# Attention scores in fp16 halves with a row of maxima: fp32 strips of 16 or 17 rows replaced by stacked 32-row strips

## The reference

```
x = x + tanh(g_xattn) * attention(layernorm(x), ctx, ctx)
    scores  = einsum('bkgsd,bktd->bkgst', qh, kh) / sqrt(16)
    weights = softmax(scores, axis=-1)
    out     = einsum('bkgst,bktd->bkgsd', weights, vh)
x = x + tanh(g_ffn) * moe(layernorm(x))
```

## Time and profile before

| | us |
|---|---|
| median of 3 runs | 1436.35 |
| lowest and highest | 1429.1, 1441.07 |
| the profiled execution | 1441.87 |
| its span | 1440.1 |

### The profile page before, as it was taken

The page is one execution under the profiler, slowest core; times in us unless marked ns, Lnnn a source line. Parts: engine busy times, 40 slices in busy tenths (PEclk is TensorE's granted clock), DMA queues, the critical chain, the costliest instruction groups (busy, mean ns, idle before and its releaser), DMA issues.

```text
span 1440.1 us, 33203 instructions
## 1 busy us (share of the span) xinstructions
PE 1353.0 (94%) x11762; PEld 989.7 (69%) x11762; DVE 878.3 (61%) x1737; ACT 519.9 (36%) x949; POOL 465.0 (32%) x373
## 2 busy tenths in 40 slices
PE   4789999999996889989999999999999999999996
PEld 3456666666652767777777777777777777777773
DVE  3767767777755886854545555544444444446887
ACT  2256656676653522222222222222222222222220
POOL 2147777777773700011111111111111111004454
PEclk9979989999985579999999999999999999999998
DMA  7224434444342741136255363546163631167666
GB/s 244 94 90 139 144 116 140 141 158 135 132 144 78 260 164 60 59 134 204 81 181 183 131 204 102 198 145 219 58 211 124 200 106 58 44 211 235 212 206 189
DMA packets 98782, 213.59 MB, mean 148 GB/s; under 512 B 10800, under 2 KB 12336, under 8 KB 98736
## 3 DMA queue, kind: packets, MB, share of 16 engines
q1 hardware_dynamic: 87536, 176.28, 36.0%
q0 software_dynamic: 11200, 36.71, 8.2%
HBM read 228.26 MB, written 66.06 MB: 204 GB/s over the span
## 4 chain that ended last, share of the span: by engine, by line
PE 89%; DVE 5%; issue 2%; DMA 2%; ACT 1%; POOL 1%; SPq 0%; DVEq 0%; ACTq 0%; POOLq 0%
PE PS L1351 38%; PE PS L1370 19%; PE PS L1193 8%; PE PS L1205 8%; PE PS L1215 5%; PE PS L1339 3%; PE PS L1226 3%; PE PS L1175 2%; DVE st L752 1%; DMA xnd<-xhl 1%; PE PS L1236 1%; PE PS L1296 1%; DVE negm L807 1%; POOL xhl L545 1%; PE PS L1164 1%
## 5 line engine op out<-in xcount | busy, mean ns | idle before, releaser
L1370 PE MATMUL PS<-wb,ghl 128*128 128x512 f16 x1296 | 293.1, 383 | 7.5 <-DVE ghl L1055 4.3
L1351 PE MATMUL PS<-xT,wb 128*128 128x256 f16 x2592 | 293.8, 274 | 1.1 <-DVE xT L1033 1.1
L1351 PE MATMUL PS<-uhl,wb 128*128 128x256 f16 x2592 | 291.8, 273 | 1.0 <-DVE uhl L1043 1.0
L1351 PEld LDWEIGHTS PS<-xT,wb 128*128 128x128 f16 x2592 | 254.5, 98 | 31.8 <-issue 1.3
L1351 PEld LDWEIGHTS PS<-uhl,wb 128*128 128x128 f16 x2592 | 251.4, 98 | 29.6 <-DVE uhl L1043 1.3
L807 DVE TENSOR_REDUCE negm<-PS 128x4 f32<-128x512 f32 x256 | 164.9, 686 | 117.5 <-PE PS L1193 114.9
L1370 PEld LDWEIGHTS PS<-wb,ghl 128*128 128x128 f16 x1296 | 127.8, 99 | 152.8 <-issue 14.1
L560 POOL COPY ixr<-idx 128x2 int32 x38 | 7.0, 184 | 606.9 <-PE PS L1339 478.2
L1205 PE MATMUL PS<-qT,kT 17*128 17x512 f32 x512 | 182.7, 690 | 16.5 <-ACT Pt L625 13.5
L625 ACT ACTIVATE Pt<-PS 128x512 f32<-128x512 f32 x256 | 140.1, 607 | 156.7 <-PE PS L1205 156.2
L1193 PE MATMUL PS<-kT,qT 16*128 16x128 f32 x2048 | 162.8, 300 | 8.0 <-DVE negm L807 8.0
(11 more groups left out here) (142 smaller groups left out, 1397.2 us busy)
## 6 DMA issues: line engine op xcount, KB each, us to landing
wb<-wsc SPq DMA_DIRECT2D x126, 1024.0 KB
wst<-in_wall SPq DMA_DIRECT2D x32, 768.0 KB, 5.6
wsc<-whl SPq DMA_DIRECT2D x32, 768.0 KB, 4.2
ysl<-yb SPq DMA_DIRECT2D x46, 512.0 KB
bd<-in_bdown SPq DMA_DIRECT2D x42, 256.0 KB
X<-in_x SPq DMA_DIRECT2D x8, 1024.0 KB, 8.8
xnd<-xhl SPq DMA_DIRECT2D x32, 256.0 KB, 2.9
xs<-xnd SPq DMA_DIRECT2D x32, 256.0 KB
```

The lines of the kernel that those rows point to most:

```text
L1351: ins = pe.matmul(bank[:, hf, (m % 2) * TT:(m % 2 + 1) * TT], wb[:, par, l, k, w, m * P:(m + 1) * P], rhs(x, k), start=(n == 0), stop=(n = ...
L1370: ins = pe.matmul(PS[2][:, t, :], ghl[:, x, k, t * P:(t + 1) * P], wb[:, par, 2, k, w, :], start=(n == 0), stop=(n == len(TERMS) - 1))
```

## The change

Queries and keys are split into fp16 halves. In a strip of 32 rows the queries now stand as 16 rows of the high half and 16 rows of the low half. The keys get two such strips: `w` = 0 has the high half twice, `w` = 1 has the low half in its first 16 rows. Two accumulating matmuls, over 32 rows and over 16, give the score. The maxima are a third pass over one row, a row of `negR` times a row of ones. They no longer go into `qT`.

The parts, by engine:

- PE: `tr_k` makes 4 fp16 transposes and `tr_q` 8 in one piece, where there were 2 and 4 + 4 in fp32. `scores_max` has 16 fp16 matmuls, and `scores_T` has 6 of 512 columns (3 passes for each of two strips). `m_done`, `t_done` and `exp_done` count whole units.
- DVE: `maxes` is one instruction of 1024. `evac_q1` is gone, `evac_k` copies 512 fp16 elements, and `norm1` (the normalised x in fp32) and `weights64` are new on it.
- ACT: `exps` is one instruction of 1024. `queries` becomes `high`, which writes `kx` and then the high half of `qx`, and it moves behind the first `exps`. `evac_q` copies all 1024 elements of `qT`.
- POOL: `weights64` leaves, and `split_kq` comes, which subtracts the high halves to get the low ones of keys and queries.
- Order: `evac_neg(nx, 0)` and its transpose move behind the third maximum, `outputs(pv, 1)` behind the second, `outputs(b, 0)` and `stats2` to the end of the body.

```
             def neg_rows(half, par, pair):
                 sp.wait_ge(S["negT_ready"], 2 * number(half, par) + pair + 1)
-                sp.dma_start(qT[D::STRIP, quad, pair, :, :], negT[:, pair, :]).then_inc(neg_in[pair], 16)
+                sp.dma_start(negR[0::STRIP, par, pair, :, :], negT[:, pair, :]).then_inc(neg_in[pair], 16)
...
+            def split_kq(half, par):
+                b = 2 * half + par
+                cv = C[:, bass.ds(b, 1), :].rearrange("p o (h d) -> p (o h) d", d=D)
+                need(g, S["tk_done"], b - 1)
+                g.wait_ge(S["kh_ready"], b + 1)
...
+                g.tensor_tensor(kx[:, par, 1, :, 0, :], cv, kx[:, par, 0, :, 0, :], ALU.subtract).then_inc(S["k_split"], 1)
+                g.wait_ge(S["qh_ready"], b + 1)
+                g.wait_ge(S["xn_ready"], b + 1)
+                xv = xn32[:, par, :].rearrange("p (k m d) -> p k m d", m=HPG, d=D)
+                g.tensor_tensor(qx[:, par, :, :, 1, :].rearrange("p m k d -> p k m d"), xv,
+                                qx[:, par, :, :, 0, :].rearrange("p m k d -> p k m d"), ALU.subtract).then_inc(S["q_split"], 1)
...
+            def high(half, par):
+                b = 2 * half + par
+                need(act, S["tk_done"], b - 1)
+                cv = C[:, bass.ds(b, 1), :].rearrange("p o (h d) -> p (o h) d", d=D)
+                act.activation(kx[:, par, 0, :, :, :], cv.unsqueeze(2).to_broadcast([P, NKV, 2, D]), ACT.Copy).then_inc(S["kh_ready"], 1)
+                need(act, S["tq_done"], b - 1)
+                act.activation(qx[:, par, :, :, 0, :].rearrange("p m k d -> p k m d"),
                                X[:, bass.ds(b, 1), :].rearrange("p o (k m d) -> p (o k) m d", m=HPG, d=D),
+                               ACT.Identity, bias=ln[:, 1, bass.ds(b, 1)], scale=ln[:, 0, bass.ds(b, 1)]).then_inc(S["qh_ready"], 1)
...
             def exps(half, par, u):
-                for odd in range(2):
-                    act.wait_ge(S["t_done"], 2 * n + odd + 1)
...
+                act.wait_ge(S["t_done"], n + 1)
+                act.activation(Pt[:, u, :, :].rearrange("p h s -> p (h s)"), Tb[:, :, :].rearrange("p o c -> p (o c)"), ACT.Exp,
+                               scale=float(D) ** -0.5).then_inc(S["exp_done"], 1)
...
             def body(half, par, quad):
...
+                exps(half, par, 0)
                 if after is not None:
-                    queries(*after[:2])
-                exps(half, par, 0)
+                    high(*after[:2])
...
+            def norm1(half, par):
+                b = 2 * half + par
+                need(v, S["q_split"], b - 1)
+                v.tensor_scalar(xn32[:, par, :], X[:, bass.ds(b, 1), :].rearrange("p o c -> p (o c)"), ln[:, 0, bass.ds(b, 1)],
+                                ln[:, 1, bass.ds(b, 1)], ALU.mult, ALU.add).then_inc(S["xn_ready"], 1)
...
+                v.wait_ge(S["m_done"], UNITS * b + u + 1)
+                v.tensor_reduce(negm[:, u // 2, u % 2 * 8:u % 2 * 8 + 8], Mb[:, :, :].rearrange("p o (m t) -> p (o m) t", t=CTX),
+                                AX.X, ALU.max, negate=True).then_inc(S["max_done"], 1)
...
             def scores_max(half, par, quad, u):
...
                 for m in range(HPG):
+                    for w, rows in ((0, STRIP), (1, D)):
+                        for odd in range(2):
+                            part = strip(u, odd, rows)
+                            ins = pe.matmul(Mb[:, odd, m * P:(m + 1) * P], qT[part, quad, u // 2, m, :], kT[part, quad, w, u // 2, :],
+                                            start=w == 0, stop=w == 1)
+                ins.then_inc(S["m_done"], 1)
...
             def scores_T(half, par, quad, u):
...
                 pe.wait_ge(neg_in[u // 2], 16 * (b + 1))
+                need(pe, S["exp_done"], UNITS * b + u)
+                for w, rows in ((0, STRIP), (1, D)):
+                    for odd in range(2):
+                        part = strip(u, odd, rows)
+                        pe.matmul(Tb[:, odd, :], kT[part, quad, w, u // 2, :], qT[part, quad, u // 2, :, :].rearrange("p m c -> p (m c)"),
+                                  start=w == 0, stop=False)
                 for odd in range(2):
+                    part = strip(u, odd, 1)
+                    ins = pe.matmul(Tb[:, odd, :], one16[part, :], negR[part, par, u // 2, :, :].rearrange("p m c -> p (m c)"),
+                                    start=False, stop=True)
+                ins.then_inc(S["t_done"], 1)
```

More of the change, by code:

```diff
@@ L661, in body @@
                 if after is not None:
[L662 removed]
+                    evac_q(*after)
                 exps(half, par, 2)
@@ L1262, in body @@
                 if after is not None:
-                    tr_k(*after)
-                if not start:
-                    outputs(*pv, 1)
+                    tr_k(*after[:2])
                 scores_T(half, par, quad, 1)
@@ L1282, in body @@
                     tr_neg(*nx[:2], 1)
-                if after is not None:
-                    tr_q(*after[:2], 1)
+                outputs(half, par, quad, 0)
             over_batches(pe, body)
```

189 lines of the change are left out of this document (83 added, 106 removed).

## The result

The changed kernel takes 1449.45 us (median of 14 runs, 1443.51 to 1462.95), the kernel before 1436.24 in the same session (14 runs, 1426.73 to 1441.29). The ratio is 1.0103, with a 95% interval of 1.0072 to 1.0135. So it is slower, as forecast, but by 13 us instead of 37, and the interval leaves open whether it is more than the 1% that the prediction calls tellable. The time lies inside the whole range of 1405 to 1520 and half a microsecond under the forecast's own 1450 to 1500. The direction was right and the size was not. The profiled execution took 1451.01 us, with a span of 1449.0.

What follows compares the result with a forecast made beforehand. Turns between engines and PE's list were taken to set the batch period, only PE being full. 1441.9 + 40 (loop) - 3 (prologue) = 1479 us as profiled, 1473 us median; range 1405 to 1520, forecast's own 1450 to 1500.

Steps and rivals of the forecast that it cites:

- The direction and its mechanism: Attention loop: PE's work per batch shrinks, the period does not, so PE loses clock; 28 batches cost +40 us.
- the announced 0.6 to 0.8: Sign that the forecast is right: mean clock of the loop at 0.6 to 0.8, against 0.94 before.
- Rival (1): Loop clock stays as before, 12% of time at 1.2 GHz: period 11.4 us, 1425 us; chance 0.2.
- rival (2): Once down, PE's clock never rises again in the loop: 14.5 us a batch, +79 us, 1512 us; chance 0.1.
- The period at 2.4 GHz: One batch of the loop at full clock takes 11.1 us (10.4 to 11.8), against 11.11 before.
- The first wait: Second scores_T queued behind tr_k, which needs kx: 2.4 us from first exponential's end to the next exponential.
- `weights64` was to end 0.8 us behind `weights_lo`: Second new wait: DVE's weights64 is blocked by POOL's weights_lo and ends at 8.25 instead of 6.1 us.
- `evac_neg` is then done at 9.65, and with 1.5 us for the DMA: Body's end: late third maximum delays the negR DMA, so the next scores_T starts at 11.2 us; ACT's path sums to 10.4.
- The period at 1.2 GHz: One batch of the loop at the low clock takes 14.5 us, summed along the same path.
- The share at 1.2 GHz: 65% of the loop's time at the low clock, against 12% before, giving 13.1 us a batch.
- The start and the end: Ahead of the loop five shorter scores_max less wider tr_q and copies, -3 us; end of loop has same turns.
- Rival (3): weights64 starts ahead of weights_lo and the clock holds: 10.4 us at full clock, 10.8 with 12% low, 1408 us; chance 0.15.

Runs made afterwards that it cites:

- e1_fill: The changed kernel plus seven unread fp16 matmuls of 128 rows a batch, five ahead of tr_k and two ahead of the last scores_T: 1420.40 us, ratio 0.9908.
- e12_fill_16: The control of e1_fill: the changed kernel with the same seven matmuls in the same places, but on 16 rows instead of 128: 1478.02 us, ratio 1.0319.
- e7_lo_fill: The edit of e2_lo_dve, last batch scaled too, with the seven matmuls of e1_fill, on the changed kernel: 1379.58 us, ratio 0.9589.
- e2_lo_dve: The changed kernel without weights64: ACT scales while writing the high half, one DVE operation makes the low half instead of POOL: 1438.83 us, ratio 1.0019.
- e8_neg_early: The changed kernel with tr_neg and evac_neg of the first pair back ahead of tr_q and weights64: 1462.45 us, ratio 1.0177.

## Why the prediction was right and wrong

In short: the way by which the change loses was right, and terms of the sum were mis-sized. The share of time at 1.2 GHz was 57% and not 65%, which put 8 us too many into the loop, and the two periods put in 6 more. The part ahead of the loop gave 11.2 us and not 3, and the end of the loop 7.9 us and not nothing. For the profiled execution 37 us were forecast and 9 came.

**The direction and its mechanism: right.** "The period doesn't shrink while PE's work per batch does, so PE does less at full rate than now." PE's busy time fell by 46 us, the period at full clock moved by 0.18 us, and the clock fell from 0.94 to 0.71, inside the announced 0.6 to 0.8. In a body wholly at full clock PE is busy for 8.1 of 10.9 us. e1_fill against e12_fill_16, and e7_lo_fill against e2_lo_dve, show that the clock is the cause of the loss. What in the change takes the clock down is less sure: the control shows that PE's busy share alone is not it, and no run isolates the fewer passes from the 16-bit numbers and the new order. One reading of the clock was not exact: the stretch ahead of the fall at 208.5 us was said to hold no output pass, but one ran from 203.63 to 204.69. Rival (1), a clock that stays, and rival (2), one that never rises again, are both out.

**The period at 2.4 GHz: right, with one link of two named.** 10.93 us for the 11.1 taken. The first wait was forecast as 2.4 us between the first two exponentials with over 1 us idle: 349.55 - 347.25 is 2.30, with 1.29 idle. `weights64` was to end 0.8 us behind `weights_lo`: 0.81. But the step "`evac_neg` is then done at 9.65, and with 1.5 us for the DMA ... the next `scores_T` starts at 11.2" named one of two chains. The landing comes last, as it says: `evac_neg` is done 9.3 us behind the body's first `scores_T`, the DMA lands 1.6 us later, and the next `scores_T` starts at 10.9. But PE's own chain behind the same late maximum ends within 0.1 us of it, which the prediction did not see, so e8_neg_early gets 0.14 us by an early landing. What both chains hang on is `weights64`; e2_lo_dve, which shortens it, gets 0.82 us and comes to 10.11, where the prediction had 10.4 without the block.

**The period at 1.2 GHz: near.** 14.27 us for 14.5. The sum to 14.5 is itself a little short: the terms listed for the stretch up to the second exponential add up to some 3.3 us, where 3.2 were taken.

**The share at 1.2 GHz: the larger part of the loop's miss.** "The change thins PE's list by less than that, so I take 65%." Measured is 57%. With my two periods that share alone gives 1 / (0.57/14.5 + 0.43/11.1) = 12.8 us instead of 13.1, which is 8 of the 14 us by which the loop was forecast too long; the two periods, each 0.2 us too long, give the other 6. The estimate rested on 13 us of two stretches near the end of the loop, where one kind of work had run out.

**The start and the end: the step that failed outright.** "-3 us" for the prologue and "the end of the loop has the same turns" for the end: measured are -11.2 and -7.9. The first was read from one row, `scores_max` at 1.2 GHz, and the second from none. Of the start, 6.4 us are gained by the first exponential (33.02 for 39.42). The five `scores_max` give 5 x 1.05 us, as forecast (2.08 and 1.03 each), and the wider `tr_q` and its copies cost 2.2 us ahead of the first of them, as forecast; but they take the place of transposes that stood between the maxima before (2.8 us), and this was not counted. Another 4.8 us are gained in the first two bodies, which I had left out. They run mostly at 1.2 GHz as well, by the length of their output passes, though the profile's clock shows 1.00 until 68.6 us before and 63.8 us now. First of before, then of after:

```profile
53.68 1.94 PE L1215 MATMUL PS<-Pt,Va 128*32 128x512 f32 x8
```

```profile
49.51 1.97 PE L1244 MATMUL PS<-Pt,Va 128*32 128x512 f32 x8
```

The end is like it: in the last two bodies of before ACT waits 2.7 to 4.1 us ahead of each second and fourth exponential, 13.7 us together; after the change no wait ahead of an exponential there is over 2.3 us. So the term to be summed was PE's saved work over everything ahead of and behind the 28 batches, and not five turns of a maximum. PE's busy time falls by 8.1 us up to the first exponential, by 8.0 in the first two bodies and by 9.2 in the last two, and the time by 6.4, 4.8 and 7.9, together 19 us. This attribution is read from the two traces; no run isolates it. Together with the loop this is the whole miss: 14 + 8.2 + 7.9 - 2.0 = 28 us, of the 37 forecast and 8.9 found.

**Rival (3), `weights64` ahead of `weights_lo` and the clock holding:** its 10.4 us at full clock and 1408 us did not come by themselves. In all 28 bodies in which POOL was at work `weights_lo` started first. What the rival described could be had by other means: with the block gone and the clock held, e7_lo_fill runs 10.09 us and 1380 us.
